# First attention of a four-stage transformer block: queries and keys packed into three products, rows placed by transfers, normalisation moved to the output

## What is computed

```
q, k, v = (xn @ Wq + bq, xn @ Wk + bk, xn @ Wv + bv)   # 2 heads of 64 features
q, k = [content 32 | rotate(spatial 32)] in each head  # rotary turn of the last 32 features
score = q @ k.T / sqrt(64)                             # per sequence and head
out = softmax(score) @ v
x = x + out @ Wo + bo
```

## Time and profile before

| | us |
|---|---|
| median of 3 runs | 713.66 |
| lowest, highest | 712.37, 716.26 |
| the profiled execution | 717.27 |
| its span, first to last instruction | 715.5 |
| the span's TensorE clock, mean share of full speed | 0.98 |

### The profile page before, as it was taken

How to read it: one execution, slowest core, us unless ns; L and a number is a source line. 1 busy time by engine, 2 the same in 40 slices (tenths; PEclk the granted TensorE clock), 3 DMA queues, 4 the chain that set the end, 5 groups by cost and what they waited for, 6 DMA issues and landing times.

```text
span 715.5 us, 14025 instructions
## 1 busy us (share of the span) xinstructions
PE 657.6 (92%) x4713; PEld 457.9 (64%) x4716; DVE 497.8 (70%) x958; ACT 450.6 (63%) x801; POOL 425.5 (59%) x443
## 2 busy tenths in 40 slices
PE   3789998689999999997999999998989999999997
PEld 1455555477777877665555555554546777787785
DVE  6769998665657768556788888885678566775521
ACT  3668887446566666545676677775765556566664
POOL 4544543267777786633345645653666777778673
PEclk9989999899999999999999999998999999999999
DMA  6101230000000000560457666663221000000000
GB/s 195 41 22 42 53 42 2 1 1 1 1 0 0 0 1 2 162 245 7 149 186 235 210 211 225 231 205 137 77 80 47 1 15 16 15 0 15 16 16 29
DMA packets 33028, 52.47 MB, mean 73 GB/s; under 512 B 4560, under 2 KB 9680, under 8 KB 32976
## 3 DMA queue, kind: packets, MB, share of 16 engines
q1 hardware_dynamic: 32784, 51.53, 23.0%
q10 hardware_dynamic: 192, 0.26, 0.1%
HBM read 27.15 MB, written 24.38 MB: 72 GB/s over the span
## 4 chain that ended last, share of the span: by engine, by line
PE 63%; DVE 14%; ACT 8%; issue 7%; DMA 4%; POOL 1%; SPq 1%; DVEq 0%; ACTq 0%; POOLq 0%
PE banks L220 60%; ACT b_prob L1525 4%; DVE xn L182 2%; DVE a_mx L652 2%; ACT a_prob L553 2%; DMA f_h_lo<-b_k_dram 2%; DMA b_o_dram<-b_o 1%; PE banks L212 1%; DVE f_gate L1088 1%; DMA b_k_dram<-b_k_lo 1%; DVE f_h_hi L1091 1%; PE banks L977 1%; DVE f_hidden L1094 1%; DVE a_prob L666 1%; ACT f_g_hi L1044 1%
## 5 line engine op out<-in xcount | busy, mean ns | idle before, releaser
L1158 POOL TENSOR_TENSOR f_g_lo<-f_gelu,f_g_hi 128x512 fp32r<-128x512 f32 x127 | 162.9, 1291 | 54.0 <-ACT f_g_hi L1044 53.4
L1043 ACT ACTIVATE f_gelu<-banks,cols 128x512 f32<-128x512 f32 x128 | 88.3, 690 | 130.6 <-PE banks L220 108.6
L1624 DVE TENSOR_REDUCE b_segment_max<-banks 128x6 f32<-128x768 f32 x128 | 120.2, 950 | 31.1 <-PE banks L220 30.4
L1741 POOL TENSOR_SCALAR_AFFINE_SELECT b_prob<-b_prob 128x512 f32<-128x512 f32 x128 | 81.6, 638 | 93.5 <-ACT b_prob L1525 92.8
L220 PE MATMUL banks<-f_g_hi,whi 128*128 128x512 f32 x320 | 130.2, 407 | 1.9 <-POOL f_g_lo L1158 1.4
L220 PE MATMUL banks<-f_g_lo,whi 128*128 128x512 f32 x320 | 126.7, 396 | 0.0
L1525 ACT ACTIVATE b_prob<-banks 128x768 f32<-128x768 f32 x128 | 102.4, 807 | 38.5 <-PE banks L220 38.2
L1151 POOL TENSOR_TENSOR f_h_lo<-f_hidden,f_h_hi 128x512 fp32r<-128x512 f32 x60 | 77.5, 1292 | 64.5 <-DVE f_hidden L1094 62.8
L220 PE MATMUL banks<-f_h_hi,whi 128*128 128x512 f32 x256 | 104.5, 408 | 5.4 <-POOL f_h_lo L1151 2.7
L220 PE MATMUL banks<-f_h_lo,whi 128*128 128x512 f32 x256 | 101.7, 397 | 0.0
L1044 ACT ACTIVATE f_g_hi<-banks,cols 128x512 fp32r<-128x512 f32 x128 | 87.4, 683 | 0.0
(11 more groups left out here) (125 smaller groups left out, 1093.6 us busy)
## 6 DMA issues: line engine op xcount, KB each, us to landing
f_h_hi<-b_q_dram SPq DMA_DIRECT2D x16, 512.0 KB, 4.0
f_h_lo<-b_k_dram SPq DMA_DIRECT2D x16, 512.0 KB, 5.0
b_o_dram<-b_o SPq DMA_DIRECT2D x8, 1024.0 KB, 4.4
b_q_dram<-b_q_hi SPq DMA_DIRECT2D x16, 256.0 KB, 3.2
b_k_dram<-b_k_hi SPq DMA_DIRECT2D x16, 256.0 KB, 3.0
w_stage<-in_wF SPq DMA_DIRECT2D x8, 352.0 KB, 3.3
b_q_dram<-b_q_lo SPq DMA_DIRECT2D x8, 256.0 KB, 3.6
b_k_dram<-b_k_lo SPq DMA_DIRECT2D x8, 256.0 KB, 3.2
```

The lines of the kernel that those rows point to most:

```text
L1043: nc.scalar.activation(gf[c % 2][:, :], z_bank[c % 2], ACT.Gelu, scale=scale).then_inc(s_gf, 1)
L1158: nc.gpsimd.tensor_tensor(lo[:, c, :], gf[c % 2][:, :], hi[:, c, :].bitcast(F32), ALU.subtract).then_inc(s_glo[c % 2], 1)
L1624: nc.vector.reduce_max(seg[:, g, s, 2 * p:2 * p + 2, :], first_pass[:, 2 * p:2 * p + 2, 0:3 * P].rearrange("p b (c k) -> p b c k", c=3), A ...
L1741: nc.gpsimd.affine_select(out=pr, in_=pr, compare_op=ALU.is_ge, fill=0.0, base=0, pattern=[[0, 4], [1, P]], channel_multiplier=-1).then_in ...
```

## The change

- Queries and keys are packed. The host orders the columns of Wq and Wk so that one product holds the content features of both heads' queries and keys (128 rows), a second the spatial ones, a third the spatial ones with swapped partners. With v that is four products instead of five. The query's share carries the scale 1/8 from the start, in the cosines, the sines and a scaled bias.
- The content rows go from PSUM to SBUF by one ACT pass (`act_content`). The spatial ones take the two DVE passes and one POOL addition, once per block instead of twice.
- The rows then lie on the wrong partitions. `sp_moves` has SP issue eight transfers per block from SBUF to SBUF, 32 rows of 512 float32 each (64 KB): four of content rows, four of spatial rows. `pe_scores` waits for both. SP's loads of weight pieces, formerly a loop of their own (`sp_split`), now stand between the moves of successive blocks.
- Probabilities aren't normalised. `pe_out` makes the projection of the two heads apart, into two banks (eight products of 64 rows by 128 columns instead of four of 128 rows), and `dve_update` adds each head's part to x with its inverse totals as scale, eight instructions per block instead of one. Those banks are the ones of the content and spatial products, so these wait for the updates.
- The maxima come negated out of the reduction; `shift` is made on POOL, with one more small multiplication there.
- Weight pieces on DVE move ahead of the update and the maxima.

```diff
-            def dve_shift(self, dve, b):
-                dve.wait_ge(self.rstd, b.t + 1)
-                dve.wait_ge(self.xn, TILES * b.t)
-                nc.vector.scalar_tensor_tensor(out=shift[:, :], in0=mv[:, :, 0], scalar=-1.0, in1=rstd[:, :],
-                                               op0=ALU.mult, op1=ALU.mult).then_inc(self.shift, 1)
+            def pool_shift(self, pool, b):
+                pool.wait_ge(self.rstd, b.t + 1)
+                nc.gpsimd.tensor_tensor(shift[:, :], nmean[:, :], rstd[:, :], ALU.mult).then_inc(self.shift, 1)
...
+                if shifted:
+                    nc.gpsimd.tensor_tensor(nmean[:, :], mv[:, :, 0], mone[:, :], ALU.mult)
                 pool.wait_ge(self.veps, t + 1)
                 pool.wait_ge(self.xn, TILES * t)
...
+            def sp_moves(sp, n):
+                t = n.t
+                wait(sp, s_sc, SEQS * (t - 1))
+                sp.wait_ge(s_co, t + 1)
+                for g in range(PIECES):
+                    h, to = g // 2, (qT, kT)[g % 2][n.odd]
+                    sp.dma_start(to[DA * h:DA * h + HALF_A, :],
+                                 content[ROWS_A * g:ROWS_A * (g + 1), :]).then_inc(s_mc, 16)
+                sp.wait_ge(s_ro, t + 1)
+                for g in range(PIECES):
+                    h, to = g // 2, (qT, kT)[g % 2][n.odd]
+                    sp.dma_start(to[DA * h + HALF_A:DA * (h + 1), :],
+                                 spatial[ROWS_A * g:ROWS_A * (g + 1), :]).then_inc(s_ms, 16)
...
+            def pe_swapped(pe, n):
+                pe.wait_ge(s_xT, n.t + 1)
+                project(misc, wA[:, W_SWAPPED, :], xnT[n.odd][:, :]).then_inc(s_wr, 1)
+            def pe_content(pe, n):
+                wait(pe, s_co, n.t)
+                project(content_bank, wA[:, W_CONTENT, :], xnT[n.odd][:, :]).then_inc(s_wc, 1)
+            def pe_spatial(pe, n):
+                wait(pe, s_st, n.t)
+                project(spatial_bank, wA[:, W_SPATIAL, :], xnT[n.odd][:, :]).then_inc(s_ws, 1)
+            def pe_v(pe, n):
+                pe.wait_ge(s_tu, n.t + 1)
+                token_major(misc, xnT[n.odd][:, :], wA[:, WV, :]).then_inc(s_v, 1)
...
             def pe_scores(pe, b, s):
                 if s == 0:
-                    pe.wait_ge(s_ro, 2 * (b.t + 1))
+                    pe.wait_ge(s_mc, 16 * PIECES * (b.t + 1))
+                    pe.wait_ge(s_ms, 16 * PIECES * (b.t + 1))
                 wait(pe, s_ex, UNITS * b.t + HA * s)
                 for qt in range(2):
...
-            def pe_out(pe, b, bank=y_bank):
+            def pe_out(pe, b, bank0=content_bank, bank1=spatial_bank):
                 pe.wait_ge(s_oc, b.t + 1)
-                token_major(bank, oT, wA[:, WO, :]).then_inc(s_y, 1)
+                for s in range(TILES):
+                    for h, bank in enumerate((bank0, bank1)):
+                        at = slice(DA * h, DA * (h + 1))
+                        last = mm(bank[:, s * P:(s + 1) * P], oT[at, s * P:(s + 1) * P], wA[at, WO, :])
+                last.then_inc(s_y, 1)
             def pe_body(pe, b, before, one, two):
                 n1, n2 = b.after(1), b.after(2)
                 nxt = link["next"]
                 pe_scores(pe, b, 1)
                 if one:
-                    pe_proj(pe, n1, "k")
-                for h in (1, 0):
+                    pe_v(pe, n1)
+                for h in range(HA):
                     pe_probT(pe, b, 0, h)
-                if one:
-                    pe_proj(pe, n1, "kr")
                 pe_pv(pe, b, 0)
-                if one:
-                    pe_proj(pe, n1, "v")
                 if before:
+                    pe.wait_ge(s_co, b.t + 2)
+                    pe.wait_ge(s_st, b.t + 2)
                     pe_out(pe, b.after(-1))
                 if one:
                     pe_scores(pe, n1, 0)
                 if two:
                     pe_T(pe, n2)
                 else:
-                    pe.wait_ge(s_tu, 2 * BLOCKS)
+                    pe.wait_ge(s_done, b.t)
                     nxt["pe_T"](pe, FIRST_BLOCK)
-                for h in (0, 1):
+                for h in range(HA):
                     pe_probT(pe, b, 1, h)
                 if two:
-                    pe_proj(pe, n2, "qr")
-                    pe_proj(pe, n2, "q")
+                    pe_swapped(pe, n2)
+                    if before:
+                        pe.wait_ge(s_half, b.t)
+                    pe_content(pe, n2)
+                    if before:
+                        pe.wait_ge(s_done, b.t)
+                    pe_spatial(pe, n2)
                 else:
                     pe.wait_ge(s_vr, BLOCKS)
                     ffn["pe_total"](pe)
...
+            def act_content(act, n):
+                act.wait_ge(s_wc, n.t + 1)
+                wait(act, s_mc, 16 * PIECES * n.t)
+                nc.scalar.activation(content[:, :], content_bank[:, :], ACT.Identity, bias=b_content[:, :],
+                                     scale=col("factor")).then_inc(s_co, 1)
...
             def act_body(act, b, before, one, two):
                 n1, n2 = b.after(1), b.after(2)
                 nxt = link["next"]
+                if before:
+                    act_out(act, b.after(-1))
                 if two and not is_block(b, 0):
                     ffn["beside"]["act"](act, n2)
-                act_normalise(act, b, 0)
-                if before:
-                    act_out(act, b.after(-1))
-                for h in (1, 0):
+                for h in range(HA):
                     act_probT(act, b, 0, h)
                 act_exp(act, b, 1)
                 if two:
                     norm.act_apply(act, n2)
-                act_normalise(act, b, 1)
-                if two:
                     act_xT(act, n2)
                 else:
                     nxt["act_xhi"](act, FIRST_BLOCK)
-                for h in (0, 1):
+                for h in range(HA):
                     act_probT(act, b, 1, h)
                 if one:
                     act_exp(act, n1, 0)
+                if two:
+                    act_content(act, n2)
                 if is_block(b, 0):
                     ffn["beside"]["act"](act, n2)
...
+            def dve_inverse(dve, b):
+                dve.wait_ge(s_ex, UNITS * (b.t + 1))
+                nc.vector.reciprocal(inv[b.odd][:, :, :, :], total[b.odd][:, :, :, :]).then_inc(s_in_, 1)
+            def dve_update(dve, b, h, bank):
                 dve.wait_ge(s_y, b.t + 1)
-                dve.wait_ge(s_bo, b.t + 1)
-                nc.vector.tensor_tensor(xblk(b.t), tiles_of(bank), xblk(b.t), ALU.add).then_inc(s_done, 1)
+                dve.wait_ge(s_in_, b.t + 1)
+                dve.wait_ge(s_half if h else s_bo, b.t + 1)
+                for s in range(TILES):
+                    x = X[:, bass.ds(TILES * b.t + s, 1), :]
+                    last = nc.vector.scalar_tensor_tensor(
+                        out=x, in0=tiles_of(bank)[:, s:s + 1, :], scalar=inv[b.odd][:, s // 2, h, s % 2:s % 2 + 1],
+                        in1=x, op0=ALU.mult, op1=ALU.add)
+                last.then_inc(s_done if h else s_half, 1)
             def dve_body(dve, b, before, one, two):
                 n1, n2 = b.after(1), b.after(2)
                 nxt = link["next"]
-                if not two:
-                    ffn["dve_total"](dve)
-                dve_inverse(dve, b, 0)
                 if two:
                     norm.dve_stats(dve, n2)
                 else:
+                    ffn["dve_total"](dve)
                     nxt["norm"].dve_stats(dve, FIRST_BLOCK)
-                dve_normalise(dve, b, 0)
                 dve_max(dve, b, 1)
-                if two:
-                    norm.dve_shift(dve, n2)
-                dve_negate(dve, b, 1)
                 if one:
-                    dve_rope(dve, n1, "k")
-                    dve_rope(dve, n1, "kr")
...
```

265 lines of the change are left out of this document (120 added, 145 removed).

## The result

The changed kernel took 727.48 us (median of four executions, 725.04 to 728.75), the kernel before 713.63 beside it: a ratio of 1.0185, interval [1.0146, 1.0224]. Run again with six executions it took 723.15 against 713.07, 1.0131 [1.0091, 1.0171]. The changed kernel is slower; the forecast was no change, 712.2 in 708 to 718. Its executions also spread, from 717.7 to 730.4, where those of the kernel before nearly all stay within 711 to 717, the highest at 719.8.

What follows compares the result with a forecast made beforehand. The prediction took attention's chain through PE, DVE and ACT, with little slack, as the bound. Its terms -2.6 + 1.3 - 2.1 + 1.1 + 0.8 = -1.5 gave 712.2 us on the median's scale, range 708 to 718.

Steps and rivals of the forecast that it cites:

- The steady body: Attention bodies between second scores of blocks 2 and 6: 12.45 us instead of 13.10, four times, -2.6.
- an unpaired projection: Rival: the output projection's 64-row products don't run in pairs, steady body stays 13.1; +2.6, 714.8 us; chance 0.11.
- late transfers in every body: Rival: the eight transfers land at 7.2 and become the wait of every body; +9.1, 721.3 us; chance 0.10.
- Transfers in sequence: Rival: the eight transfers follow each other in full, landing 11.6 into the body; +40, 752 us; chance 0.04.
- The rule of the Trainium skill: Transfers to different partition ranges don't run beside each other and small ones should be merged; taken literally, 752 us.
- The start, +1.3: Block 0's first scores wait for transfers, 22.3 instead of 20.31: +2.0, of which 0.7 comes back in body 0.
- the prediction's own sign: If the start costs over 3 us, or the steady body is well under 12.3, the account of the body is wrong.
- 0.7 comes back in body 0: Body 0's chain is shortened like that of the other bodies, returning 0.7 of the start's +2.0.
- Body 1, -2.1: Body 1 takes 15.9 instead of 17.98, as transposes no longer need DVE; first-half scores run at 47.75.
- The clock, +1.1: PE idles 2.4 us in body 1 and 2.1 in body 6, so the clock may fall there; from 0 to 3.5.
- The last blocks, 0: Body 6 and block 7 lose scalings but wait for the update instead: nothing, from -0.5 to +0.5.
- The hand-over, +0.8: Block 7's update takes DVE 2.0 us instead of 0.68 in the first feed-forward body: +0.8, bounds 0 and 1.3.

Runs made afterwards that it cites:

- the second execution: The second profiled execution of the unaltered changed kernel, at 718.81 us; the first was at 725.04.
- the filled kernels: Changed kernel with PE's idle time filled by products nobody reads: 728.88 us alone, 718.49 when the second attention's constants are also sent later.
- the bank experiment: Changed kernel with the second head's projection of body 6 in another bank, so the feed-forward's transposes don't wait for the update of x: 718.22 us.
- late constants: Changed kernel with SP sending the second attention's constants only when all eight blocks have updated x: 719.60 us, ratio 1.0083 to the kernel before.
- the kernel with all repairs: Changed kernel with late constants, body 6's second bank, reordered start and DVE's first weight pieces moved: 709.88 us, 0.9950 of the kernel before.
- the start's order: Late constants plus block 0's content rows from ACT's queue and first scores, maxima and exponentials ahead of block 1's products and passes: 721.24 us.
- the pieces: DVE counts weight pieces of blocks 0 and 1 in body 0, 2 and 3 in body 1; added to late constants, start's order and bank: 715.32 to 709.88.

## Why the prediction was wrong

- **The steady body** was right: 12.45 foreseen, 12.36 to 12.64 in bodies 3 to 5. So were its steps: in body 3 values times probabilities, next scores, the norm's transposes, the three products and the last values start at 4.0, 6.2, 7.3, 8.7 and 11.6 for 3.9, 5.9, 7.3, 8.7 and 11.4. So were its parts: the projection of 64 rows paired (16 records, and in the kernel without transfers the scores start 1.00 behind them), PE idle 0.8 to 0.9 before the values. The rivals on it did not happen: an unpaired projection, and late transfers in every body (of bodies 2 to 5 the scores wait for one in body 2, 1.84, and in body 4, 0.28). Transfers in sequence, 752, were far off: eight issued 0.63 apart land 2.0 after their own issue, so three are in flight at a time. The rule of the Trainium skill that the prediction cites is, in its literal form, not what these rows show. (The prediction calls what DVE lost 1.4; the two scalings are 2.6 together. The sum doesn't use it.)
- **Body 2** is the steady body that failed, 15.63. The term took a landing of 2.4 after issue with a slack of 0.4; the real issue of 0.63 instead of 0.50 had used up the slack (landings 6.2 to 6.3 into the body, needed at 5.9), and the packet of instructions then cost 1.6 and the clock behind it 1.1. With the second execution's landing the four bodies came out at -1.9, for -2.6 foreseen.
- **The start, +1.3**, was the largest failure in the trace: +5.2 by the second scores of block 1, and past the prediction's own sign that a start of over 3 us makes its account wrong. First scores came at 23.8 instead of 22.3, through content ready at 17.2 instead of 16.3 and the longer issues. But the step that failed is "0.7 comes back in body 0". I shortened that body like the others and didn't ask what had filled PE between the two scores of block 0 before. It was block 1's products, which the change moves in front of the first scores. PE then idled 3.35 there, the clock fell, and body 0 took 15.0 instead of 13.1. The wait as such cost nothing, since first and second scores are 4.5 apart and were 4.7 apart before. The clock did: with the gap filled the body takes 12.4, and the 0.7 does come back.
- **Body 1, -2.1**, was right: -1.6 in the trace, with the scores 8.3 into the body as foreseen and DVE's two waits of 3.0 for pieces. (The terms given for its 47.75 add up to 47.57.)
- **The clock, +1.1** was put in two places. In body 1 it held after 2.15; in body 6 it fell in one execution and held in the other. It fell at the start, in body 2 and in the last block as well. So the places were wrong, and in the traces the size too: the fall in body 0 alone cost 2.3 to 2.6. By the medians of the filled kernels all falls together cost 1.1; the two don't agree.
- **The last blocks, 0**, were mis-sized: body 6 took 16.5 and 15.0 instead of 13.8. I had written that the transposes would wait for the update and then costed the body at nothing; the bank experiment shows 13.2 without that wait and 3 to 5 us less over all. With the constants late as well it is 11.7 to 11.9.
- **The hand-over, +0.8**: 11.9 for 12.0 from the values of block 7 to the first hidden product, so nothing. (Both at a low clock; where it holds, 9.0 to 9.1 in either order.)
- **The missing term.** The wording of the change has SP's loads "between the moves of successive blocks", and I followed the weight pieces but not what stands behind them on the same queue. The constants came 36 us later, onto the flag and the branch. What late constants gave, between 1.8 and 7.9 us, belongs to no step of the sum; the profiles show 1.4 of it, in front of the flag.

Against the changed kernel's second median of 723.15 the kernel with all repairs gives 13.3 back, of which late constants are 3.6, the start's order by itself nothing (1.6 slower), the bank 5.9 and the pieces 5.4, in this order of steps; other orders were not run. That is more than the loss of 10.1, since the pieces are not the change's alone: a piece held body 1 in the kernel before as well. So the set shows that the loss lies in attention A's waits and in the constants, and its division is less sure. Left open: which executions meet the accident at the branch, how many of the changed kernel's above 724 do (the one that was profiled doesn't), and what the falls of the clock cost over many executions.

## What to carry to other kernels

Follow a queue to its end: a transfer added in front of others moves all that stand behind it, and the question is what they now run beside. When an order changes, ask for each pair of dependent instructions what used to lie between them, since the same chain without that work is a wait. A bank that two stages share is a wait, and is to be costed as one.

## What the runs showed of the hardware

- Instructions come by DMA, most of them in packets of 16 KB that take 0.9 to 1.9 us each. One of them delayed a 64 KB transfer from 2.0 to 3.6 us, and one in each of nine profiles started only as the kernel's constants ended. PE's stand at one branch was between 0.84 and 3.07 us in most profiles, and 7.49 and 10.89 us in two; it ended 1.6 to 1.8 us after such a packet in all 17.
- The same idle time of PE, 2.35 us at the same place, was followed by the level of 1.2 GHz in one execution (granted clock 0.50) and by 2.4 GHz in another of the same kernel (1.00).
- SP needs 0.63 us from one issue to the next for transfers of 32 rows from SBUF to SBUF.
